# Per-language adapter with layer norm: each batch's W1 copied on chip and held stationary, x ring of nine pairs, one scaling per pair moved off VectorE

## The chip, the core and the metric

The kernel runs on one core of one Trainium2 chip. The metric is the device time of one execution in microseconds, the median of several. TensorE (PE) does the matrix products, VectorE (DVE), ScalarE (ACT) and GpSimd (POOL) the elementwise work, and SyncE (SP) issues nearly all DMAs. GpSimd can't read the matmul banks (PSUM); VectorE and ScalarE can. In this document a *pair* is two batches; there are 64.

## The reference, cut to what matters

There are 128 batches of x, each 128 rows by 512 columns, and ten languages. Every batch has a language id, which picks its W1 (512 x 128), b1, W2 (128 x 512), b2, gamma and beta. All is float32.

```python
h = relu(einsum('bsh,bha->bsa', x, W1[ids]) + b1[ids])
y = x + einsum('bsa,bah->bsh', h, W2[ids]) + b2[ids]
mean, var = mean(y, -1), var(y, -1)
out = x + (y - mean) * rsqrt(var + 1e-5) * gamma[ids] + beta[ids]
```

## The kernel before

All tables of all ten languages stay on chip in SBUF; the language of a batch is a register value that each engine loads from `lang_ids` (L156 to L160) and uses as an offset into the tables. Per pair the work goes like this.

- SP (L206 to L250) loads x of a pair (512 KB, `x_io`, a ring of 24 slots, that is 12 pairs) and stores the result from the same slots. In the steady state it waits for `out_ready` of pair p, issues the store, then waits for the store of pair p - 1 and issues the load of pair p + 11 (L239 to L244).
- PE, step p (L455 to L476): the second product of pair p - 3 (`second_product`, L420, three matmuls of 512 columns per batch, float32 split into a high and a low part: h_high x W2_high, h_high x W2_low, h_low x W2_high), the eight transposes of x of pair p + 1 (`turn_x`, L388), the two transposes of h of pair p - 1 (`turn_h`, L407), and the first product of pair p (`first_product`, L397). There x_T is the stationary operand and W1, at an offset from a register, the moving one, so h comes out with rows in partitions and has to be transposed. Each batch starts with a bf16 matmul that brings b1 (L399).
- ACT, step p (L351, L379 to L385): squares with their sum for both banks of pair p - 3 and the square root (`square_pair`, L343), the copy of transposed x out of PSUM (`copy_x`, L318), the copy of h before it is transposed (`copy_h`, L331, with the relu) and of its high part after (`high_h`, L336).
- DVE (`norm_and_seed`, L599): for pair n it scales both banks, (y - mean) x gamma, in place in PSUM (`scale_pair`, L559), inverts the deviation (L564), finishes both batches, bank x rstd + x, into x's slots (`finish_pair`, L572), makes the low part of h of pair n + 2 (`low_h`, L529), and seeds the banks of pair n + 2 with x + b2, with the row sum (`seed_pair`, L540; inputs `x_io` and `b2_all`, both in SBUF). There are four banks `ps_y`, two pairs' worth.
- POOL (`add_beta`, L288): for pair n it waits for both seeds and for the transposes of x, makes the two means (L292), and adds beta to x in its slots, twice (L295; inputs `x_io` and `beta_all`).

So DVE's order is written out by hand, and PE, ACT, POOL and SP follow it through semaphores. Before that there is a prologue of about 37 us, in which the tables are loaded, gamma and beta are spread to all partitions by matmuls (L438), and W2 is made free of its mean and split in two parts. `w2_high` is made by ACT (L328), `w2_low` by DVE (`low_w2`, L520, from the staged W2 and `w2_high`, both in SBUF). POOL cuts beta and b2 into three bf16 parts in that time (`cut_in_three`, L271).

Of the kernel before, what the change touches and what calls it, by code (L numbers as in the profile page):

```python
# [13 lines left out]
SLOTS = 24  # L14
Y_BANKS = 4
H_PAIRS = 6
FIRST = 3
# [4 lines left out]
def build(nc, x, ids, w1, b1, w2, b2, gamma, beta, out):  # L22
# [11 lines left out]
    x_pairs = x.rearrange("(n b) s h -> s n b h", b=2)  # L34
    out_pairs = out.rearrange("(n b) s h -> s n b h", b=2)
# [6 lines left out]
    assert FIRST + 2 <= H_PAIRS  # L42

    with ExitStack() as ctx:  # L44
# [10 lines left out]
        w1_all = sb("w1_all", [128, L, C, A], F32)  # L55
        w2_high = sb("w2_high", [128, L, H], F32R)
# [9 lines left out]
        cut = sb("cut", [128, 3, H], BF16)  # L66
# [4 lines left out]
        b1_parts = sb("b1_parts", [128, A], BF16)  # L71
        later_part = sb("later_part", [128, 2], F32)
# [3 lines left out]
        ids_raw = sb("ids_raw", [1, B], I32)  # L76
        ids_fix = sb("ids_fix", [1, 2, B], F32)
        lang_ids = sb("lang_ids", [1, B], I32)
        eps = sb("eps", [128, 1], F32)
        over_h = sb("over_h", [128, L], F32)  # L80
# [4 lines left out]
        h_rows = sb("h_rows", [128, 2, 2, A], F32)  # L85
# [4 lines left out]
        mean = sb("mean", [128, SLOTS], F32)  # L90
# [6 lines left out]
        ps_h = psum("ps_h", [128, H], F32)  # L97
        ps_hT = psum("ps_hT", [128, H], F32)
# [8 lines left out]
        s_w1 = sem("s_w1")  # L107
        s_w2 = [sem(f"s_w2_{n}") for n in range(W_CHUNKS)]
# [8 lines left out]
        over_h_ready = sem("over_h_ready")  # L117
# [27 lines left out]
        h_rows_ready = sem("h_rows_ready")  # L145
        h_turned = sem("h_turned")
# [46 lines left out]
        spread_banks = ps_y + [ps_h, ps_hT]  # L193
# [13 lines left out]
        def _(sp):  # L207
# [3 lines left out]
            sp.dma_start(ids_raw[:, :], ids.rearrange("(a b) -> a b", a=1)).then_inc(s_ids, 16)  # L211
# [7 lines left out]
            for n in range(W2_AHEAD):  # L219
                load_w2(n)  # L220
# [9 lines left out]
            for p in range(4, X_FIRST):  # L230
# [3 lines left out]
                load_x(p)  # L234
            for n in range(W_CHUNKS):
# [17 lines left out]
        def _(pool):  # L253
# [5 lines left out]
            for g in range(3):  # L259
                nc.gpsimd.affine_select(out=pick_row[:, :], in_=pick_row[:, :], compare_op=ALU.not_equal, fill=1.0,  # L260
                                        base=-L * g, pattern=[[-1, L]], channel_multiplier=1).then_inc(pick_step, 1)
                pool.wait_ge(pick_step, g + 1)

# [4 lines left out]
            nc.gpsimd.memset(over_h[:, :], 1.0 / H).then_inc(over_h_ready, 1)  # L268
            nc.gpsimd.memset(neg_over_h[:, :], -1.0 / H).then_inc(over_h_ready, 1)
# [12 lines left out]
            pool.wait_ge(parts_zero, 2)  # L282
# [5 lines left out]
            def add_beta(n):  # L288
                langs = langs_of(pool, n)
                pool.wait_ge(seeded, 2 * n + 2)  # L290
                pool.wait_ge(x_turned, 2 * n + 2)
                nc.gpsimd.tensor_tensor(stats(mean, n), stats(row_sum, n), over_h[:, 0:2], ALU.mult).then_inc(mean_ready, 1)  # L292
                for b in range(2):
                    t = 2 * n + b
                    nc.gpsimd.tensor_tensor(x_slot(t), x_slot(t), of_lang(beta_all, langs[b]), ALU.add)\  # L295
                        .then_inc(x_beta_ready, 1)

            pool.wait_ge(ids_ready, 1)
            pool.wait_ge(over_h_ready, 2)
            pool.wait_ge(spread_act, len(by_act))  # L300
            pool.wait_ge(spread_dve, len(by_dve))
            for n in range(PAIRS):
                add_beta(n)

        @block.scalar
        def _(act):
# [24 lines left out]
            def copy_h(p):  # L331

                act.wait_ge(h_summed, p + 1)
                nc.scalar.activation(flat(h_rows[:, p % 2, :, :]), pair_of(ps_h), ACT.Relu).then_inc(h_rows_ready, 1)  # L334

            def high_h(p):  # L336
                act.wait_ge(h_turned, p + 1)
                if p >= H_PAIRS:
                    act.wait_ge(adapted, 2 * (p - H_PAIRS) + 2)
                nc.scalar.copy(flat(h_high[:, p % H_PAIRS, :, :]), pair_of(ps_hT)).then_inc(h_high_ready, 1)  # L340
# [9 lines left out]

            def step(p):  # L351
# [3 lines left out]
                if p > 0:  # L355
                    high_h(p - 1)
                copy_h(p)
# [14 lines left out]
            copy_h(0)  # L372
            copy_x(2)
            high_h(0)
            high_w2(3)
            copy_h(1)
            high_w2(4)
            step(2)
            for p in range(FIRST, PAIRS):  # L379
                square_pair(p - FIRST)  # L380
                step(p)
            square_pair(PAIRS - FIRST)
            high_h(PAIRS - 1)
            for n in range(PAIRS - FIRST + 1, PAIRS):
                square_pair(n)  # L385

        @block.tensor
        def _(pe):  # L388
            def turn_x(t):
                if t % 2 == 0:  # L390
                    pe.wait_ge(x_loaded[t // 2 % X_PAIRS], x_loads(t // 2))
                for c in range(C):
                    last = nc.tensor.transpose(ps_T[:, t % 2, c, :], x_io[:, t % SLOTS, c * 128:(c + 1) * 128],  # L393
# [3 lines left out]
            def first_product(t, lang):  # L397
                part = pair_of(ps_h)[:, (t % 2) * A:(t % 2 + 1) * A]
                nc.tensor.matmul(part, of_lang(pick, lang), b1_parts[:, :], start=True, stop=False)  # L399
                for c in range(C):  # L400
                    last = nc.tensor.matmul(part, x_T[:, t % 4, c, :],  # L401
                                            w1_all[:, bass.ds(lang, 1), c, :].rearrange("p o a -> p (o a)"),
                                            start=False, stop=(c == C - 1))
                if t % 2 == 1:
                    last.then_inc(h_summed, 1)

            def turn_h(p):  # L407
                pe.wait_ge(h_rows_ready, p + 1)
                if p > 0:
                    pe.wait_ge(h_low_ready, p)  # L410
                for b in range(2):
                    last = nc.tensor.transpose(pair_of(ps_hT)[:, b * S:(b + 1) * S], h_rows[:, p % 2, b, :],  # L412
                                               identity[:, :])
                last.then_inc(h_turned, 1)
# [21 lines left out]
            pe.wait_ge(parts_zero, 2)  # L436
# [14 lines left out]
            pe.wait_ge(b1_parts_ready, 1)  # L451
            pe.wait_ge(spread_act, len(by_act))
            pe.wait_ge(spread_dve, len(by_dve))
            pe.wait_ge(s_w1, 16 * W_CHUNKS)
            for p in range(PAIRS):  # L455
# [10 lines left out]
                if p > 0:  # L466
                    turn_h(p - 1)
                for b in range(2):
                    first_product(2 * p + b, langs[p][b])
# [7 lines left out]
            for n in range(PAIRS - FIRST, PAIRS):  # L477
                for b in range(2):
                    second_product(2 * n + b, langs[n][b])
                if n == PAIRS - FIRST:  # L480
                    turn_h(PAIRS - 1)

        @block.vector
        def _(dve):
            nc.vector.memset(parts[:, :], 0.0).then_inc(parts_zero, 1)
            nc.vector.memset(b1_parts[:, :], 0.0).then_inc(parts_zero, 1)
            dve.wait_ge(s_ids, 16)
# [16 lines left out]

            dve.wait_ge(later_part_ready, 1)
            dve.wait_ge(parts_zero, 2)
# [126 lines left out]
```

## Time and profile before

| what | value |
|---|---|
| median of 3 runs | 325.21 us (325.19 to 325.84) |
| the profiled execution, first to last instruction (span) | 323.8 us |
| around the span, against the median | 1.4 us |
| PE busy | 301.9 us, 93% |
| DVE busy | 307.6 us, 95% |
| ACT busy | 230.4 us, 71% (a square: 0.69 us, 128 of them) |
| POOL busy | 185.7 us, 57% |
| DMA | 75.7 MB, 234 GB/s on average |

The span is what the profiler saw from the first to the last instruction; the execution's own time isn't given separately, so the prediction sums up to the span and adds what lies between it and the median. Busy times of PE count matmuls that overlap in the pipeline as one. An idle time in a row is that of the engine just before the operation, with what ended it behind the arrow. Starts of neighbouring operations tell what each costs; records overlap a little.

### The profile page before, as it was taken

The numbers are of one execution on the slowest core, as the hardware profiler recorded it, in microseconds if no ns is written. First come the engines' busy times: TensorE is split into PE (matmuls) and PEld (weight loads), VectorE is DVE, ScalarE is ACT, GpSimd is POOL, SyncE is SP. The second block draws the span as 40 slices with busy tenths as digits, with TensorE's granted clock in tenths as the row PEclk, the third lists the DMA queues.
The fourth block names the chain that finished last, engine by engine and source line by source line (L and its number), as shares of the span: only waits on it lengthen the run. The fifth ranks groups of instructions, "written<-read, shape, count | busy, mean of one in ns | idle before, by whom it ended". The sixth has DMA issues, their size and how long they took to land. (4 is left out here: it accounts for less than half of the span.)

```text
span 323.8 us, 8068 instructions
## 1 busy us (share of the span) xinstructions
PE 301.9 (93%) x2200; PEld 272.8 (84%) x2200; DVE 307.6 (95%) x679; ACT 230.4 (71%) x541; POOL 185.7 (57%) x217
## 2 busy tenths in 40 slices
PE   1659999999999999999999999999999999999962
PEld 1239899999999999999999999999999999999941
DVE  5687999999999999999999999999999999999996
ACT  3956677777777777877778777787777877778752
POOL 2960755556655566555665556655566555665553
PEclk9877999999999999999999999999999999999995
DMA  5999988766766667676776676766667666433324
GB/s 160 302 356 428 379 291 273 236 228 231 257 232 227 228 229 263 223 233 226 230 256 232 228 231 227 261 236 221 231 225 262 221 234 232 160 132 134 130 108 152
DMA packets 41711, 75.69 MB, mean 234 GB/s; under 512 B 2253, under 2 KB 7404, under 8 KB 41542
## 3 DMA queue, kind: packets, MB, share of 16 engines
q1 hardware_dynamic: 41571, 75.04, 68.5%
q8 instruction: 21, 0.34, 0.4%
q14 instruction: 20, 0.16, 0.1%
q10 hardware_dynamic: 99, 0.14, 0.1%
HBM read 41.62 MB, written 33.55 MB: 232 GB/s over the span
## 5 line engine op out<-in xcount | busy, mean ns | idle before, releaser
L295 POOL TENSOR_TENSOR x_io<-x_io,beta_all 128x512 f32<-128x512 f32 x128 | 161.2, 1280 | 0.0
L401 PE MATMUL ps_h<-w_all,x_T 128*128 x1024 | 137.0, 284 | 0.0
L401 PEld LDWEIGHTS ps_h<-w_all,x_T 128*128 128x128 f32 x1024 | 126.1, 194 | 1.6
L345 ACT ACTIVATE cut<-ps_y,row_sum 128x512 bf16<-128x512 f32 x128 | 88.0, 688 | 24.0 <-PE ps_y L428 24.0
L572 DVE SCALAR_TENSOR_TENSOR x_io<-ps_y,rstd,x_io 128x512 f32<-128x512 f32 x128 | 90.2, 747 | 2.5 <-DVE rstd L564 0.3
L559 DVE SCALAR_TENSOR_TENSOR ps_y<-ps_y,mean,gamma_all 128x512 f32<-128x512 f32 x128 | 90.8, 754 | 0.8 <-ACT cut L345 0.6
L292 POOL TENSOR_TENSOR mean<-row_sum,over_h 128x2 f32<-128x2 f32 x64 | 12.9, 201 | 125.6 <-DVE ps_y L540 113.6
L540 DVE SCALAR_TENSOR_TENSOR ps_y<-x_io,b_all 128x512 f32<-128x512 f32 x124 | 83.1, 713 | 0.0
L393 PE MATMUL ps_T<-identity,x_io 128*128 128x128 f32 x512 | 68.2, 277 | 10.0 <-DMA x_io<-in_x 10.0
L393 PEld LDWEIGHTS ps_T<-identity,x_io 128*128 128x128 f32 x512 | 61.1, 143 | 19.1 <-issue 10.4
L322 ACT COPY x_T<-ps_T 128x1024 f32<-128x1024 f32 x64 | 63.7, 995 | 8.2 <-PE ps_T L393 8.2
L334 ACT ACTIVATE h_rows<-ps_h 128x256 f32<-128x256 f32 x64 | 24.8, 387 | 52.0 <-PE ps_h L401 52.0
L428 PE MATMUL ps_y<-w_high,h_high 128*128 x128 | 56.4, 440 | 3.4 <-DVE ps_y L540 3.0
L428 PE MATMUL ps_y<-w_high,h_low 128*128 x128 | 51.1, 399 | 0.0
L428 PE MATMUL ps_y<-w_low,h_high 128*128 x128 | 50.9, 398 | 0.0
L428 PEld LDWEIGHTS ps_y<-w_high,h_high 128*128 128x128 f32 x128 | 24.5, 192 | 7.1 <-issue 4.2
L428 PEld LDWEIGHTS ps_y<-w_high,h_low 128*128 128x128 f32 x128 | 24.3, 190 | 5.7
L529 DVE SCALAR_TENSOR_TENSOR h_low<-ps_hT,h_high 128x256 fp32r<-128x256 f32 x64 | 26.6, 415 | 1.9 <-ACT h_high L340 1.9
L399 PE MATMUL ps_h<-b_parts,pick 128*128 128x128 bf16 x128 | 28.2, 220 | 0.0
L428 PEld LDWEIGHTS ps_y<-w_low,h_high 128*128 128x128 f32 x128 | 24.6, 192 | 2.6
L345 ACT ACTIVATION_READ_ACCUMULATOR cut<-ps_y,row_sum 128x1 f32 x128 | 24.6, 192 | 0.0
L412 PE MATMUL ps_hT<-identity,h_rows 128*128 128x128 f32 x128 | 24.5, 273 | 0.1
(60 smaller groups left out, 173.6 us busy)
## 6 DMA issues: line engine op xcount, KB each, us to landing
x_io<-in_x SPq DMA_DIRECT2D x64, 512.0 KB, 4.4
out<-x_io SPq DMA_DIRECT2D x63, 512.0 KB, 3.0
x_io<-in_L_cond_W SPq DMA_DIRECT2D x5, 512.0 KB, 7.2
w_all<-in_L_cond_W SPq DMA_DIRECT2D x5, 512.0 KB, 8.9
b_all<-in_L_cond_b SPq DMA_DIRECT2D x1, 2560.0 KB, 15.7
out<-x_io SPq DMA_DIRECT2D x2, 256.0 KB, 2.0
x_io<-in_L_cond_gamma SPq DMA_DIRECT2D x1, 60.0 KB
x_io<-in_L_cond_beta ACTq DMA_DIRECT2D x1, 60.0 KB
```

Of the source, the lines that this page charges most:

```text
L295: nc.gpsimd.tensor_tensor(x_slot(t), x_slot(t), of_lang(beta_all, langs[b]), ALU.add)\
L322: nc.scalar.copy(x_T[:, slots, :, :].rearrange("p b c s -> p (b c s)"), ps_T[:, :, :, :].rearrange("p b c s -> p (b c s)")).then_inc(x_T_r ...
L334: nc.scalar.activation(flat(h_rows[:, p % 2, :, :]), pair_of(ps_h), ACT.Relu).then_inc(h_rows_ready, 1)
L345: nc.scalar.activation(squares[:, t % 2, :], ps_y[t % Y_BANKS][:, :], ACT.Square, scale=-float(H), bias=stat(row_sum, t), accum_out=stat(s ...
L393: last = nc.tensor.transpose(ps_T[:, t % 2, c, :], x_io[:, t % SLOTS, c * 128:(c + 1) * 128], identity[:, :])
L399: nc.tensor.matmul(part, of_lang(pick, lang), b1_parts[:, :], start=True, stop=False)
L401: last = nc.tensor.matmul(part, x_T[:, t % 4, c, :], w1_all[:, bass.ds(lang, 1), c, :].rearrange("p o a -> p (o a)"), start=False, stop=(c ...
L428: last = nc.tensor.matmul(bank, h_part[:, h, b, :], of_lang(w2_part, lang), start=False, stop=False, skip_group_check=True)
L529: nc.vector.scalar_tensor_tensor(flat(h_low[:, p % H_PAIRS, :, :]), pair_of(ps_hT), 1.0, flat(h_high[:, p % H_PAIRS, :, :]).bitcast(F32), ...
L540: nc.vector.scalar_tensor_tensor(ps_y[t % Y_BANKS][:, :], x_slot(t), 1.0, of_lang(b2_all, langs[b]), ALU.mult, ALU.add, accum_out=stat(row ...
L559: nc.vector.scalar_tensor_tensor(bank, bank, stat(mean, t), of_lang(gamma_all, langs[b]), ALU.subtract, ALU.mult).then_inc(scaled, 1)
L572: nc.vector.scalar_tensor_tensor(x_slot(t), ps_y[t % Y_BANKS][:, :], stat(rstd, t), x_slot(t), ALU.mult, ALU.add).then_inc(out_ready, 1)
```

## The change

W1 is now read from HBM so that partition p holds rows 4p to 4p + 3 of each language's W1, in one run of 2 KB. The transposes of x pick every fourth column to match (column 4p + c of x goes to partition p of part c). SP copies the W1 of each batch from the table `w1_all` to one of eight slots `w1_stage` (four pairs), two DMAs of 256 KB per pair, six pairs ahead. In the first product the slot is the stationary operand and x_T the moving one, so h comes out already transposed, with relu put into the copy of the high part and into the low part. `copy_h` and `turn_h` are gone, and there are two banks `ps_h`. One bf16 matmul per pair brings b1, with its moving operand a table `is_lang` of ones and zeros that is spread over 256 columns. The ring of x has 18 slots, the second product runs 2 steps behind instead of 3.

DVE scales only the first bank of a pair. For the second, ACT writes y - mean to SBUF (`centred`, two slots), POOL multiplies it by gamma in place, and DVE finishes from there, one pair later. The seed of a second bank then waits for the centring and not for the finish. POOL's order per pair is the means, beta for the first batch, gamma for the second of the pair before, beta for the second batch.

```diff
-SLOTS = 24
+SLOTS = 18
-H_PAIRS = 6
-FIRST = 3
+H_PAIRS = 3
+STAGE_PAIRS = 4
+STAGE_AHEAD = 6
+FIRST = 2
+    w1_rows = w1.rearrange("l (p c) a -> p l c a", c=C)
...
+            def stage_w1(q):
+                langs = langs_of(sp, q)
+                if q >= STAGE_PAIRS:
+                    sp.wait_ge(h_summed, q - STAGE_PAIRS + 1)
+                for b in range(2):
+                    sp.dma_start(w1_stage[:, 2 * (q % STAGE_PAIRS) + b, :, :], w1_all[:, bass.ds(langs[b], 1), :, :])\
+                        .then_inc(w1_staged[q % STAGE_PAIRS], 16)
...
-                sp.dma_start(w1_all[:, langs, :, :], w1[langs].rearrange("l (c p) a -> p l c a", p=128)).then_inc(s_w1, 16)
+                sp.dma_start(w1_all[:, langs, :, :], w1_rows[:, langs, :, :]).then_inc(s_w1, 16)
+            sp.wait_ge(ids_ready, 1)
+            sp.wait_ge(s_w1, 16 * W_CHUNKS)
+            stage_w1(0)
             load_x(1)
+            stage_w1(1)
             for n in range(W2_AHEAD, W_CHUNKS):
                 load_w2(n)
             load_x(2)
-            load_x(3)
+            stage_w1(2)
+            stage_w1(3)
             sp.dma_start(b2_all[:, :, :], b2.partition_broadcast(128)).then_inc(s_b2, 16)
...
             for p in range(PAIRS - 1):
+                if p + STAGE_AHEAD < PAIRS:
+                    stage_w1(p + STAGE_AHEAD)
                 sp.wait_ge(out_ready, 2 * p + 2)
...
-            def add_beta(n):
+            def add_beta(t, lang):
+                pool.wait_ge(x_turned, t + 1)
+                nc.gpsimd.tensor_tensor(x_slot(t), x_slot(t), of_lang(beta_all, lang), ALU.add).then_inc(x_beta_ready, 1)
+
+            def gain(n, lang):
+                pool.wait_ge(centred_ready, n + 1)
+                nc.gpsimd.tensor_tensor(centred[:, n % 2, :], centred[:, n % 2, :], of_lang(gamma_all, lang), ALU.mult)\
+                    .then_inc(gained, 1)
...
             for n in range(PAIRS):
-                add_beta(n)
+                langs[n] = langs_of(pool, n)
+                mean_of_pair(n)
+                add_beta(2 * n, langs[n][0])
+                if n > 0:
+                    gain(n - 1, langs[n - 1][1])
+                add_beta(2 * n + 1, langs[n][1])
+            gain(PAIRS - 1, langs[PAIRS - 1][1])
...
+            def centre(n):
+                t = 2 * n + 1
+                act.wait_ge(adapted, t + 1)
+                act.wait_ge(mean_ready, n + 1)
+                if n >= 2:
+                    act.wait_ge(out_ready, 2 * (n - 2) + 2)
+                nc.scalar.activation(centred[:, n % 2, :], ps_y[t % Y_BANKS][:, :], ACT.Identity,
+                                     bias=stat(neg_mean, t)).then_inc(centred_ready, 1)
...
-                    last = nc.tensor.transpose(ps_T[:, t % 2, c, :], x_io[:, t % SLOTS, c * 128:(c + 1) * 128],
+                    last = nc.tensor.transpose(ps_T[:, t % 2, c, :], x_slot(t).rearrange("s (p c) -> s c p", c=C)[:, c, :],
                                                identity[:, :])
...
+            def first_products(p):
+                bank = pair_of(ps_h[p % 2])
+                if p >= 2:
+                    pe.wait_ge(h_low_ready, p - 1)
+                nc.tensor.matmul(bank.rearrange("a (b s) -> a b s", b=2), b1_parts[:, :],
+                                 is_lang[:, 2 * p:2 * p + 2].unsqueeze(2).broadcast_to([128, 2, S]), start=True, stop=True)
+                pe.wait_ge(w1_staged[p % STAGE_PAIRS], 32 * (p // STAGE_PAIRS + 1))
                 for b in range(2):
+                    for c in range(C):
+                        last = nc.tensor.matmul(bank[:, b * S:(b + 1) * S],
+                                                w1_stage[:, 2 * (p % STAGE_PAIRS) + b, c, :],
+                                                x_T[:, (2 * p + b) % 4, c, :],
+                                                start=False, stop=False, skip_group_check=True)
+                last.then_inc(h_summed, 1)
...
+            def finish_second(n):
+                t = 2 * n + 1
+                dve.wait_ge(rstd_ready, n + 1)
+                dve.wait_ge(gained, n + 1)
+                dve.wait_ge(x_beta_ready, t + 1)
+                nc.vector.scalar_tensor_tensor(x_slot(t), centred[:, n % 2, :], stat(rstd, t), x_slot(t),
+                                               ALU.mult, ALU.add).then_inc(out_ready, 1)
...
+            def norm_and_seed(n):
+                scale_first(n, langs[n][0])
                 if n + 2 < PAIRS:
                     langs[n + 2] = langs_of(dve, n + 2)
+                if n > 0:
+                    finish_second(n - 1)
                 invert_pair(n)
+                finish_first(n)
                 if n + 2 < PAIRS:
                     seed_pair(n + 2, langs[n + 2])
+                    low_h(n + 2)
```

## Rows read from the trace of the kernel before

**Rows 1.** Windows: busy us (count) of PE, PEld, DVE, ACT, POOL; clock, DMA share, GB/s.

```profile
32.00:48.00 16.00, 15.63 (x121) 14.48 (x120) 15.14 (x36) 12.12 (x28) 10.46 (x12) 1.00 0.92 341
60.00:270.00 210.00, 210.00 (x1590) 194.27 (x1589) 207.83 (x467) 155.57 (x373) 124.70 (x140) 1.00 0.70 235
```

**Rows 2.** Timeline of one pair, all engines: start us, us, engine, line, what.

```profile
151.83 0.48 PE L428 MATMUL ps_y<-w_high,h_high 128*128 x1
...
153.31 1.04 PE L393 MATMUL ps_T<-identity,x_io 128*128 128x128 f32 x8
...
153.79 1.42 DVE L559 SCALAR_TENSOR_TENSOR ps_y<-ps_y,mean,gamma_all 128x512 f32<-128x512 f32 x2
153.94 0.19 POOL L292 TENSOR_TENSOR mean<-row_sum,over_h 128x2 f32<-128x2 f32 x1 [1.83 <-DVE ps_y L540]
...
154.09 2.51 POOL L295 TENSOR_TENSOR x_io<-x_io,beta_all 128x512 f32<-128x512 f32 x2
...
154.18 0.38 PE L412 MATMUL ps_hT<-identity,h_rows 128*128 128x128 f32 x2
...
154.40 0.22 PE L399 MATMUL ps_h<-b_parts,pick 128*128 128x128 bf16 x1
...
155.11 0.16 DVE L564 RECIPROCAL rstd<-std 128x2 f32<-128x2 f32 x1
...
156.32 0.48 PE L428 MATMUL ps_y<-w_high,h_high 128*128 x1
...
156.96 0.69 DVE L540 SCALAR_TENSOR_TENSOR ps_y<-x_io,b_all 128x512 f32<-128x512 f32 x1
```

**Rows 3.** Timeline of DVE: first scaling, and the last two pairs.

```profile
37.01 0.76 DVE L559 SCALAR_TENSOR_TENSOR ps_y<-ps_y,mean,gamma_all 128x512 f32<-128x512 f32 x1 [0.55 <-ACT cut L345]
...
315.42 1.41 DVE L559 SCALAR_TENSOR_TENSOR ps_y<-ps_y,mean,gamma_all 128x512 f32<-128x512 f32 x2
...
319.76 1.41 DVE L572 SCALAR_TENSOR_TENSOR x_io<-ps_y,rstd,x_io 128x512 f32<-128x512 f32 x2
```

**Rows 4.** Groups of POOL, 60 to 270 us: busy us, mean ns, idle before, releaser.

```profile
L295 POOL TENSOR_TENSOR x_io<-x_io,beta_all 128x512 f32<-128x512 f32 x94 | 118.0, 1276 | 0.0
L292 POOL TENSOR_TENSOR mean<-row_sum,over_h 128x2 f32<-128x2 f32 x46 | 9.0, 195 | 84.4 <-DVE ps_y L540 84.4
```

**Rows 5.** Timeline of PE in the prologue: the first eight transposes.

```profile
6.51 1.94 PE L393 MATMUL ps_T<-identity,x_io 128*128 128x128 f32 x8 [6.51 <-DMA x_io<-in_x]
```

**Rows 6.** The page, part 6: the DMA of x and its landing.

```profile
x_io<-in_x SPq DMA_DIRECT2D x64, 512.0 KB, 4.4
```

**Rows 7.** Timelines of POOL and DVE in the prologue, single operations in order of time.

```profile
16.02 1.15 POOL L277 TENSOR_TENSOR b_rows<-b_rows,b_cut 30x512 f32<-30x512 f32 x1
...
18.19 0.74 DVE L523 SCALAR_TENSOR_TENSOR w_low<-x_io,w_neg_mean,w_high 128x512 fp32r<-128x512 f32 x1
...
18.89 1.70 POOL L277 TENSOR_TENSOR b_rows<-b_rows,b_cut 30x512 f32<-30x512 f32 x1
...
19.51 1.64 DVE L523 SCALAR_TENSOR_TENSOR w_low<-x_io,w_neg_mean,w_high 128x512 fp32r<-128x512 f32 x1
...
33.68 0.58 POOL L292 TENSOR_TENSOR mean<-row_sum,over_h 128x2 f32<-128x2 f32 x1 [12.07 <-DVE ps_y L550]
...
34.12 0.75 DVE L523 SCALAR_TENSOR_TENSOR w_low<-x_io,w_neg_mean,w_high 128x512 fp32r<-128x512 f32 x1
...
34.22 1.79 POOL L295 TENSOR_TENSOR x_io<-x_io,beta_all 128x512 f32<-128x512 f32 x1
```

**Rows 8.** Window at the end, columns as in rows 1, and PE's last wait.

```profile
306.00:324.00 18.00, 8.80 (x42) 6.19 (x39) 15.03 (x32) 7.66 (x23) 7.98 (x9) 0.73 0.39 145
...
315.04 0.77 PE L428 MATMUL ps_y<-w_high,h_high 128*128 x1 [2.79 <-DVE ps_y L540]
```

**Rows 9.** Timeline of SP's issues of W1, and DVE's sum of the third W2 chunk.

```profile
4.14 10.56 SPq L223 DMA_DIRECT2D w_all<-in_L_cond_W  x5
...
22.91 1.22 DVE L515 TENSOR_REDUCE w_sum<-x_io 128x2 f32<-128x1024 f32 x1 [0.75 <-DMA x_io<-in_L_cond_W]
```

More of the change, by code:

```diff
@@ L55, in build @@
         w1_all = sb("w1_all", [128, L, C, A], F32)
+        w1_stage = sb("w1_stage", [128, 2 * STAGE_PAIRS, C, A], F32)
         w2_high = sb("w2_high", [128, L, H], F32R)
@@ L96, in build @@
         ps_T = psum("ps_T", [128, 2, C, S], F32)
-        ps_h = psum("ps_h", [128, H], F32)
-        ps_hT = psum("ps_hT", [128, H], F32)
+        ps_h = [psum(f"ps_h{i}", [128, H], F32) for i in range(2)]
         ps_y = [psum(f"ps_y{i}", [128, H], F32) for i in range(Y_BANKS)]
@@ L107, in build @@
         s_w1 = sem("s_w1")
+        w1_staged = [sem(f"w1_staged{i}") for i in range(STAGE_PAIRS)]
         s_w2 = [sem(f"s_w2_{n}") for n in range(W_CHUNKS)]
@@ L227, in _ @@
             load_x(2)
-            load_x(3)
+            stage_w1(2)
+            stage_w1(3)
             sp.dma_start(b2_all[:, :, :], b2.partition_broadcast(128)).then_inc(s_b2, 16)
-            for p in range(4, X_FIRST):
+            for p in range(3, X_FIRST):
                 if p == ROWS_PAIR:
@@ L234, in _ @@
                 load_x(p)
+            for q in range(STAGE_PAIRS, STAGE_AHEAD):
+                stage_w1(q)
             for n in range(W_CHUNKS):
@@ L286, in _, with mean_of_pair @@
             cut_in_three(b2_rows[:, :], b2_cut[:, 1, :], parts[0:3 * L, 2 * H:3 * H], 4, b2_parts_ready)
-            def add_beta(n):
-                langs = langs_of(pool, n)
+            def mean_of_pair(n):
                 pool.wait_ge(seeded, 2 * n + 2)
[L291 to L296, printed above, removed]
+                nc.gpsimd.tensor_tensor(stats(neg_mean, n), stats(row_sum, n), neg_over_h[:, 0:2], ALU.mult)\
+                    .then_inc(mean_ready, 1)
+            def add_beta(t, lang):
[5 more added lines that the diff above has]
+                    .then_inc(gained, 1)
             pool.wait_ge(ids_ready, 1)
-            pool.wait_ge(over_h_ready, 2)
+            pool.wait_ge(neg_over_h_ready, 1)
             pool.wait_ge(spread_act, len(by_act))
             pool.wait_ge(spread_dve, len(by_dve))
+            langs = {}
             for n in range(PAIRS):
-                add_beta(n)
+                langs[n] = langs_of(pool, n)
[5 more added lines that the diff above has]
+            gain(PAIRS - 1, langs[PAIRS - 1][1])
         @block.scalar
@@ L371, in _ @@
             high_w2(2)
-            copy_h(0)
-            copy_x(2)
             high_h(0)
             high_w2(3)
-            copy_h(1)
+            copy_x(2)
+            high_h(1)
             high_w2(4)
-            step(2)
             for p in range(FIRST, PAIRS):
                 square_pair(p - FIRST)
+                centre(p - FIRST)
                 step(p)
-            square_pair(PAIRS - FIRST)
-            high_h(PAIRS - 1)
-            for n in range(PAIRS - FIRST + 1, PAIRS):
+            for n in range(PAIRS - FIRST, PAIRS):
                 square_pair(n)
+                centre(n)
         @block.tensor
@@ L465, in _ @@
                     turn_x(2 * p + 3)
[L466 to L469, printed above, removed]
+                first_products(p)
                 if p < PAIRS - 1:
@@ L551, in seed_early, with scale_first @@
                                                    accum_out=stat(row_sum, t)).then_inc(seeded, 1)
-            def scale_pair(n, langs):
+            def scale_first(n, lang):
+                t = 2 * n
+                bank = ps_y[t % Y_BANKS][:, :]
                 dve.wait_ge(mean_ready, n + 1)
-                for b in range(2):
-                    t = 2 * n + b
-                    bank = ps_y[t % Y_BANKS][:, :]
-                    dve.wait_ge(squared, t + 1)
-                    nc.vector.scalar_tensor_tensor(bank, bank, stat(mean, t), of_lang(gamma_all, langs[b]),
-                                                   ALU.subtract, ALU.mult).then_inc(scaled, 1)
+                dve.wait_ge(squared, t + 1)
+                nc.vector.scalar_tensor_tensor(bank, bank, stat(neg_mean, t), of_lang(gamma_all, lang),
+                                               ALU.add, ALU.mult).then_inc(scaled, 1)
             def invert_pair(n):
```

119 lines of the change are left out of this document (55 added, 64 removed).

## The prediction

> **What bounds the kernel now.** I read the page's busy shares first, then the windows by stage, one pair's timeline, and POOL's groups with their idle time. In the long middle two engines are full: PE is busy 210.0 of 210 us and DVE 207.8, while ACT has 155.6, POOL 124.7 and the DMA engines 0.70 [rows 1]. The timeline of one pair [rows 2] shows the period: the second product starts at 151.83 and again at 156.32, so a pair takes 4.49 us on both engines. The span agrees: the first scaling starts at 37.01, that of pair 62 at 315.42, and 62 periods of 4.49 are 278.4 us [rows 3]. So the time is 37.0 us of start, 62 periods, and 8.4 us of end, 323.8 us together; the median of the runs, 325.21, is 1.4 us more, which I add at the end.
>
> The reader should look at one more thing: what POOL does with its idle time. In the middle it waits 84.4 us for DVE's seeds [rows 4]. In the pair of [rows 2] its chain starts at 153.94, right behind the seeds, and is over at 156.60, just before DVE's next seeds start at 156.96. So the seeds, DVE operations with both inputs in SBUF, never run beside a POOL operation. The other big DVE operations of the pair take one input from PSUM.
>
> **The change, part by part.**
> PE: two transposes of h go: from 154.18 to 154.40, 0.22 us [rows 2]. Of two b1 matmuls one is left, with 256 moving columns. Sixteen products and two b1 take 154.40 to 156.32, 1.92 us; at the transposes' spacing of 0.11 (0.87 for eight) the products are 1.76, so a b1 matmul is some 0.08. The merged one costs between one and two of these: I take 0.05 saved (bounds 0 and 0.08). The sixteen products swap operands, same count, same 128 columns. PE: 4.49 - 0.27 = 4.22. The transposes of x now read every fourth element; no row has such a read, so its bounds are nothing and a halved rate: eight transposes in 1.94 us in the prologue against 1.04 in the pair [rows 2, 5]. I take nothing, the price of the nearest row of the same instruction, and keep 0.9 for the range.
> DVE: scaling two banks is 153.79 to 155.11, 1.32 us; one goes, 0.66. The other finish only changes its input from bank to SBUF. DVE: 4.49 - 0.66 = 3.83.
> ACT: loses the 0.39 us of h_rows, gains the centring, priced by the squares: 155.6 us over 46.8 pairs is 3.33. The squares are 0.69 by the trace's table in the section on the profile, so 3.63 us a pair, not the bound.
> POOL: now 2.66 us a pair (0.15 for the mean and 2.51 for two additions of beta); one more operation of the same form at 1.25 makes 3.91.
> DMA: a pair moves 1.05 MB now and 1.57 MB with the two W1 slices. At the rate of the fullest stretch shown (341 GB/s at a share of 0.92, so 371) that is 4.24 us; at the rate of the middle (235 at 0.70, so 336) it is 4.68 [rows 1]. I take 4.24, because a queue that is never empty is the first case. On SP the W1 slices are issued six pairs ahead and the loads of x seven or eight, both over 15 us against a landing of 4.4 us [rows 6], so the ring of 9 costs nothing; if that cover were gone a pair would wait those 4.4 us. The slices' two issues and language loads are priced by the 10.56 us of five W1 issues [rows 9] at most, 4.2 us for two, likelier tenths; nothing on SP is late by either, as it works pairs ahead.
>
> Alone, then, the period would be 4.3. What decides against it is how POOL and DVE run together. **The collision.** The new finish reads `centred` and x, both in SBUF; the seeds still do. The trace has such pairs in the prologue, in w2_low (both inputs in SBUF) beside POOL [rows 7]. Alone w_low takes 0.75 us. The third one started at 19.51, under a POOL tensor_tensor that ran 18.89 to 20.60, and took 1.64, so it began its work at 20.40, 0.19 before POOL's end. That POOL operation took 1.70 where its like took 1.15 (it started under the second w_low). The small mean took 0.58 where 0.20 is usual, and the first beta addition 1.79 instead of 1.28 [rows 4], ending 0.52 later because the w_low at 34.12 ran until 34.87. So each waits for nearly all of the other. Against it stands one case: the first w_low ran at its usual 0.74 beside a POOL tensor_scalar; the new work is all tensor_tensor.
> The Trainium skill, SBUF — State Buffer, Who interferes with whom, states that a VectorE instruction with two SBUF inputs and a GpSimd one that reads SBUF take turns for the whole instruction. By its whole instruction the period would be the serial sum of the second rival below; the rows agree but for the small overlap at each change of hands.
>
> Price: when DVE's operation slips between two of POOL's, POOL's counts 1.28 - 0.19 = 1.09 and DVE's 0.74 - 0.14 = 0.60 (POOL began 0.14 before w_low's end, 34.73 against 34.87). Together 1.69 against 1.25 for POOL alone: each costs 0.44. A pair has three, two seeds and the new finish, and POOL has no free time left to avoid them: 3.91 + 3 x 0.44 = 5.23. DVE fits that order: after each of its three it finds 0.85 to 1.0 us of other work (low_h and scaling, or inversion and finish) while POOL's takes 1.09. I take 5.25. PE at 4.22 of it idles 1 us a pair; its granted clock was full from 32 to 48 us [rows 1] and fell from 2.4 to 1.2 GHz at the end, around an idle of 2.79 us (0.73 on average there) [rows 8], so I leave it at full speed; at half speed nothing here would hold.
>
> Start: W1 in 2 KB rows makes its five issues shorter than the 10.56 us of before, which end at 14.70, and x of pair 1 stood behind them [rows 9]. Now SP waits for all of W1 and issues the first slices before it. 4.2 MB stand ahead in the queue, 11.3 us at 371 GB/s from 2.8, so it goes on at 14 to 16. Behind that wait stand x1, three W2 chunks and b2. The third W2 chunk then has four transfers of 1.4 us, landing near 22 to 23, and it was first used at 22.91. I keep 37.0, within 2 us.
> End: pairs 62 and 63 have no seeds. POOL does 0.15 + 4 x 1.25 and one slip of 0.44, DVE the last finish 0.75, and from the end of the last finish (321.17) to the span's end were 2.66: 9.0 us.
> **Sum**: 37.0 + 62 x 5.25 + 9.0 = 371.5, with 1.4 it is 373.
>
> **The rivals.**
> 1. No collision between these (faster): the seeds and the new finish run beside POOL freely, for instance because what was seen holds for w_low alone. Then 4.3, PE and DMA: 37.0 + 266.6 + 8.6 (no slip) + 1.4 = 314. If only the new finish collides, POOL has 4.35 and the time is 317. It decides below a period of 4.48, where the sum is that of now. For: the seeds write PSUM, and no row has one beside POOL. Against: what they share with w_low is both inputs in SBUF, and four operations of the prologue agree. Chance 0.17.
> 2. Serial: hand-overs don't alternate, or overlap nothing: 3.91 + 3 x 0.66 = 5.89, 413 us. For: POOL's next operation starts 0.03 before the last ends and may come first. Against: the rows' overlap. Chance 0.12.
> 3. DMA: 4.68 a pair, 337 us, if the collision is slight. For: three streams on one queue, share 0.70 now. Against: the full stretch. Chance 0.05.
> 4. Strided transposes: PE 4.22 + 0.9 = 5.1, 363 us. Only this and the collision together leave about the forecast. Chance 0.06 as the one that decides. The Trainium skill, SBUF — State Buffer, Door 1, says that reads which go to a new 16-byte line each time pay; four fp32 apart is such a step, and no run so far shows it.
> 5. Partly colliding, landing within 0.2% of now (what a measurement can tell): 0.03.
>
> **How the numbers follow.** The forecast has 0.57: slower in total 0.57 + 0.12 + 0.05 + 0.06 = 0.80; faster 0.17, same 0.03. The range takes rivals 3 and 4 at its low end and 2 at its high end: 336 to 414.
>
> **What the profile after would show.** Right: period 5.2 to 5.3; POOL busy (its waits counted in) near 100%; L540's successors and the new finish over 1 us instead of 0.71 and 0.75; beta additions 1.4 to 1.8 instead of 1.28; PE idle about 1 us a pair, waiting for seeds or low h; DMA share about 0.8. Wrong: those operations at their old durations; PE full at 4.2 (rival 1), or full at 5.1 with transposes 0.22 apart (4); DMA share 1 with PE waiting for w1_stage (3).

## The result, and the profile after

The changed kernel takes 401.19 us (median of 4 runs, 400.69 to 401.78) against 325.23 for the kernel before on the same chip: 1.2325 times as long, with an interval of 1.2303 to 1.2347. The prediction was 373 us, with a range of 336 to 414.

The middle first: windows of the kernel after, with the columns of [rows 1].

```profile
60.00:270.00 210.00, 169.91 (x1166) 152.96 (x1167) 199.97 (x339) 136.51 (x302) 183.62 (x152) 1.00 0.80 283
```

PE went from 210 to 170, POOL rose from 125 to 184, and the DMA engines have 0.80. DVE is recorded busy for 200, but an operation that another engine holds up counts as busy for all of that time, so this is no measure of its work. The clock stayed at the higher level of 2.4 GHz (granted share 1.00), although PE now waits in each pair. The groups of the same stretch (columns of [rows 4]) name the operations that grew:

```profile
L323 POOL TENSOR_TENSOR x_io<-x_io,beta_all 128x512 f32<-128x512 f32 x76 | 116.5, 1533 | 0.0
L588 DVE SCALAR_TENSOR_TENSOR ps_y<-x_io,b_all 128x512 f32<-128x512 f32 x75 | 88.5, 1221 | 8.7 <-DVE x_io L618 8.7
L328 POOL TENSOR_TENSOR centred<-centred,gamma_all 128x512 f32<-128x512 f32 x38 | 66.0, 1736 | 0.0
L626 DVE SCALAR_TENSOR_TENSOR x_io<-centred,rstd,x_io 128x512 f32<-128x512 f32 x38 | 45.6, 1200 | 0.0
...
L618 DVE SCALAR_TENSOR_TENSOR x_io<-ps_y,rstd,x_io 128x512 f32<-128x512 f32 x38 | 28.6, 751 | 1.4
...
L318 POOL TENSOR_TENSOR neg_mean<-row_sum,neg_over_h 128x2 f32<-128x2 f32 x38 | 7.4, 195 | 27.1 <-DVE ps_y L588 27.1
```

The seed (L588) is the same instruction as before's L540 and now takes 1.22 us on average. The finish from SBUF (L626) takes 1.20, the finish from a bank (L618) still 0.75. Gamma on POOL takes 1.74. POOL nevertheless waits 27.1 us for the second seed; its busy time and this wait fill the whole stretch, as the prediction's sign of being right had it. The timeline of one pair, DVE, POOL and PE, shows how (start us, us, engine, line, what):

```profile
200.20 1.19 DVE L626 SCALAR_TENSOR_TENSOR x_io<-centred,rstd,x_io 128x512 f32<-128x512 f32 x1
...
200.80 1.74 POOL L328 TENSOR_TENSOR centred<-centred,gamma_all 128x512 f32<-128x512 f32 x1
...
202.47 0.70 DVE L588 SCALAR_TENSOR_TENSOR ps_y<-x_io,b_all 128x512 f32<-128x512 f32 x1 [0.22 <-DVE x_io L618]
202.50 1.79 POOL L323 TENSOR_TENSOR x_io<-x_io,beta_all 128x512 f32<-128x512 f32 x1
...
203.09 1.76 DVE L588 SCALAR_TENSOR_TENSOR ps_y<-x_io,b_all 128x512 f32<-128x512 f32 x1
...
204.78 0.41 DVE L574 SCALAR_TENSOR_TENSOR h_low<-ps_h,h_high 128x256 fp32r<-128x256 f32 x1
204.99 0.19 POOL L318 TENSOR_TENSOR neg_mean<-row_sum,neg_over_h 128x2 f32<-128x2 f32 x1 [0.69 <-DVE ps_y L588]
...
205.14 1.28 POOL L323 TENSOR_TENSOR x_io<-x_io,beta_all 128x512 f32<-128x512 f32 x1
...
205.44 0.50 PE L468 MATMUL ps_y<-w_high,h_high 128*128 x1 [1.06 <-DVE h_low L574]
...
205.77 1.20 DVE L626 SCALAR_TENSOR_TENSOR x_io<-centred,rstd,x_io 128x512 f32<-128x512 f32 x1
```

L626 starts at 200.20 and again at 205.77: the period is 5.57 us. Three DVE operations with both inputs in SBUF (L626 and two of L588) take turns with three large POOL operations. The second seed ran 1.76 because it could begin only when POOL's beta ended. POOL then stood idle for 0.69 us, because its next operation, the mean, needs that very seed. PE waited 1.06 us for the low part of h, which stands behind the seed on DVE.

Start and end, DVE's timeline:

```profile
27.41 1.22 DVE L560 TENSOR_REDUCE w_sum<-x_io 128x2 f32<-128x1024 f32 x1 [5.87 <-DMA x_io<-in_L_cond_W]
...
43.86 0.75 DVE L606 SCALAR_TENSOR_TENSOR ps_y<-ps_y,neg_mean,gamma_all 128x512 f32<-128x512 f32 x1
...
389.28 0.74 DVE L606 SCALAR_TENSOR_TENSOR ps_y<-ps_y,neg_mean,gamma_all 128x512 f32<-128x512 f32 x1
```

The first scaling starts at 43.86 instead of 37.01 [rows 3], that of pair 62 at 389.28: 62 periods of 5.571. From there to the end are 9.6 us. 43.9 + 62 x 5.571 + 9.6 = 398.9, the span. Against before's span of 323.8 the 75.1 us more are 67.0 of period, 6.9 of start and 1.2 of end.

### The profile page after: what moved, and what is told of

It is laid out like the page before. It is cut to its first block and busy times, and to the rows that moved or that the text cites. A ratio compares the mean times of both kernels' runs of the same rounds, so it can differ in the third digit from the quotient of the medians.

```text
span 398.9 us, 7375 instructions
## 1 busy us (share of the span) xinstructions
PE 302.7 (76%) x2007; PEld 267.0 (67%) x2008; DVE 365.2 (92%) x619; ACT 250.2 (63%) x541; POOL 324.3 (81%) x281
## 5 line engine op out<-in xcount | busy, mean ns | idle before, releaser
L323 POOL TENSOR_TENSOR x_io<-x_io,beta_all 128x512 f32<-128x512 f32 x128 | 195.4, 1526 | 0.0
L588 DVE SCALAR_TENSOR_TENSOR ps_y<-x_io,b_all 128x512 f32<-128x512 f32 x124 | 147.9, 1234 | 13.9 <-DVE x_io L618 13.9
L450 PE MATMUL ps_h<-x_T,w_stage 128*128 128x128 f32 x1024 | 126.9, 278 | 0.0
L450 PEld LDWEIGHTS ps_h<-x_T,w_stage 128*128 128x128 f32 x1024 | 121.5, 195 | 0.8
L328 POOL TENSOR_TENSOR centred<-centred,gamma_all 128x512 f32<-128x512 f32 x64 | 110.1, 1720 | 0.9 <-ACT centred L395 0.9
L436 PEld LDWEIGHTS ps_T<-identity,x_io 128*128 128x128 f32 x512 | 73.1, 209 | 21.5 <-issue 16.5
L626 DVE SCALAR_TENSOR_TENSOR x_io<-centred,rstd,x_io 128x512 f32<-128x512 f32 x64 | 76.0, 1188 | 1.0 <-POOL centred L328 0.9
L618 DVE SCALAR_TENSOR_TENSOR x_io<-ps_y,rstd,x_io 128x512 f32<-128x512 f32 x64 | 48.1, 751 | 2.3
L606 DVE SCALAR_TENSOR_TENSOR ps_y<-ps_y,neg_mean,gamma_all 128x512 f32<-128x512 f32 x64 | 47.6, 744 | 0.3 <-ACT cut L382 0.3
L395 ACT ACTIVATE centred<-ps_y,neg_mean 128x512 f32<-128x512 f32 x64 | 42.7, 668 | 0.0
L574 DVE SCALAR_TENSOR_TENSOR h_low<-ps_h,h_high 128x256 fp32r<-128x256 f32 x64 | 26.5, 414 | 0.0
```

The lines of the kernel that those rows point to most:

```text
L328: nc.gpsimd.tensor_tensor(centred[:, n % 2, :], centred[:, n % 2, :], of_lang(gamma_all, lang), ALU.mult)\
L395: nc.scalar.activation(centred[:, n % 2, :], ps_y[t % Y_BANKS][:, :], ACT.Identity, bias=stat(neg_mean, t)).then_inc(centred_ready, 1)
L436: last = nc.tensor.transpose(ps_T[:, t % 2, c, :], x_slot(t).rearrange("s (p c) -> s c p", c=C)[:, c, :], identity[:, :])
L450: last = nc.tensor.matmul(bank[:, b * S:(b + 1) * S], w1_stage[:, 2 * (p % STAGE_PAIRS) + b, c, :], x_T[:, (2 * p + b) % 4, c, :], start=F ...
L588: nc.vector.scalar_tensor_tensor(ps_y[t % Y_BANKS][:, :], x_slot(t), 1.0, of_lang(b2_all, langs[b]), ALU.mult, ALU.add, accum_out=stat(row ...
L606: nc.vector.scalar_tensor_tensor(bank, bank, stat(neg_mean, t), of_lang(gamma_all, lang), ALU.add, ALU.mult).then_inc(scaled, 1)
```

## The experiments

Each was compared with the kernel before on the same chip, except the small kernel without an adapter, which ran once. "Period" is a 62nd of the time from the first scaling to that of pair 62. The edits are shortened; names in a row and words in brackets stand for the lines of the change.

**The split of the scaling alone.** The kernel before, with only the second scaling divided among ACT, POOL and DVE as in the change (ring of 11 pairs to make room for `centred`).

```diff
-SLOTS = 24
+SLOTS = 22
-scale_pair / finish_pair / add_beta
+scale_first, finish_second(n - 1), finish_first, centre, gain   (as in the change)
```

> The kernel before with only the scaling of the second bank moved (centring on ScalarE, gamma on GpSimd, finish from SBUF one pair later), no W1 slots, ring of 11 pairs, low h ahead of the seeds. Theory: taking turns costs the same as in the changed kernel, 5.2 to 5.6 us a pair, 370 to 398 us, with second seed, new finish and gamma long. Rival A: near 325, PE at 4.49. Rival B: near 325.

400.76 us, ratio 1.2287 (1.2228 to 1.2346), period 5.68; the expected range ended at 398. This half alone makes the whole loss, with a DMA share of only 0.56. Its start is that of before (first scaling at 37.17), and its period is 0.11 longer than the changed kernel's, so that the two times agree only by chance to 0.4 us. Its groups of DVE and POOL in the middle:

```profile
L573 DVE SCALAR_TENSOR_TENSOR ps_y<-x_io,b_all 128x512 f32<-128x512 f32 x74 | 90.3, 1259 | 0.3 <-issue 0.3
...
L303 POOL TENSOR_TENSOR centred<-centred,gamma_all 128x512 f32<-128x512 f32 x37 | 63.7, 1722 | 0.0
L611 DVE SCALAR_TENSOR_TENSOR x_io<-centred,rstd,x_io 128x512 f32<-128x512 f32 x37 | 57.0, 1540 | 0.0
```

**The W1 half alone.** The changed kernel with both scalings and finishes back on DVE.

```diff
-scale_first, finish_second(n - 1), finish_first, centre, gain
+scale_pair, finish_pair, both betas on POOL   (as before the change)
```

> The W1 half of the change alone: slots, swapped operands, ring of 9, but both scalings of a pair on VectorE and only two beta additions on GpSimd. Theory (VectorE operations with both inputs in SBUF and GpSimd's take turns): the long operations go away, the seeds are at 0.7 us again and GpSimd's at 1.28. VectorE has its 4.49 us plus the 0.22 us that the seed now waits right behind the finish: 4.7 us a pair, 335 to 342 us. Rival A (the W1 copies, half as much DMA again, slow the operations): seeds and beta additions stay long, above 380 us. Rival B (the change's PE order and low h after the seeds are what costs): above 380 us too, with operations at their old durations.

330.23 us, ratio 1.0144 (1.0097 to 1.019), period 4.43, below the expected 335 to 342; the 0.22 us of waiting that was expected in each pair did not come. Both rivals wanted above 380 us and fall. With `low_h` ahead of the seeds:

```diff
-                    seed_pair(n + 2, langs[n + 2])
-                    low_h(n + 2)
+                    low_h(n + 2)
+                    seed_pair(n + 2, langs[n + 2])
```

> As w1_only, with low h ahead of the seeds as in the kernel before. Theory: the 0.22 us wait in front of the first seed is covered again; VectorE bound at 4.43 to 4.49 us a pair, PE at 4.35: 320 to 327 us. Rival A: above 380. Rival B: near 325, but then w1_only must be above 380.

329.1 us, ratio 1.0106 (1.0061 to 1.0151), period 4.425. The period is the expected one; the time is 2 us above its range, which the late start below accounts for. Its window, and SP's issues in the prologue:

```profile
60.00:270.00 210.00, 209.89 (x1485) 192.13 (x1484) 208.31 (x477) 146.22 (x336) 126.41 (x142) 1.00 1.01 354
```

```profile
4.13 3.36 SPq L241 DMA_DIRECT2D w_all<-in_L_cond_W  x5
18.44 1.21 SPq L234 DMA_DIRECT2D w_stage<-w_all  x2
```

So the W1 half gains only 0.07 us a pair, since DVE's own work is 4.42 against PE's former 4.49. It loses 7.2 us at the start (first scaling at 44.21): SP waits from 7.5 to 18.44 for the whole of W1. The DMA engines ran at 354 GB/s and a share of 1.01 without anybody waiting for them in the middle.

**The copies.** The changed kernel without W1 copies past the first four pairs; later pairs use the slices of the first four. It leaves out 120 of the 128 copies.

```diff
-            for q in range(STAGE_PAIRS, STAGE_AHEAD):
-                stage_w1(q)
...
-                if p + STAGE_AHEAD < PAIRS:
-                    stage_w1(p + STAGE_AHEAD)
...
-                pe.wait_ge(w1_staged[p % STAGE_PAIRS], 32 * (p // STAGE_PAIRS + 1))
+                pe.wait_ge(w1_staged[p % STAGE_PAIRS], 32)
```

> The changed kernel without the W1 copies after the first four pairs; later pairs use the W1 of those four, so that part of the computation is not the reference's. Theory: within 1% of the changed kernel, 397 to 403 us, same long operations. Rival A: near or below 325 us.

401.0 us, ratio 1.2294, period 5.58, DMA share 0.56. The copies cost the changed kernel nothing in the middle.

**POOL's multiplication away.** The changed kernel without `gain`; the second finish waits for the centring. Gamma is left out for every second batch.

```diff
-                if n > 0:
-                    gain(n - 1, langs[n - 1][1])
-                dve.wait_ge(gained, n + 1)
+                dve.wait_ge(centred_ready, n + 1)
```

> The changed kernel without GpSimd's multiplication by gamma for the second batch of each pair (left out of the result); the new finish, from SBUF, stays. Theory: GpSimd has 2.66 us and at most three changes of hands at 0.44, 3.98 a pair, VectorE 3.83 + 0.22 and one or two blocked operations: 4.4 to 4.9 us a pair, 320 to 352 us. Rival B (order of low h and PE's wait for it): no change, near 400 us.

340.31 us, ratio 1.0414 (1.0377 to 1.0451), period 4.61, the median one 4.55. Its groups:

```profile
L323 POOL TENSOR_TENSOR x_io<-x_io,beta_all 128x512 f32<-128x512 f32 x92 | 136.5, 1504 | 0.2 <-issue 0.2
...
L585 DVE SCALAR_TENSOR_TENSOR ps_y<-x_io,b_all 128x512 f32<-128x512 f32 x92 | 62.0, 715 | 10.4 <-DVE x_io L615 10.4
L623 DVE SCALAR_TENSOR_TENSOR x_io<-centred,rstd,x_io 128x512 f32<-128x512 f32 x45 | 52.6, 1168 | 1.9 <-POOL x_io L323 0.7 <-issue 0.6
```

With POOL free again in part of the pair, the seeds are back at 0.715 us. What collides is the finish from SBUF, which slips between the two betas. The middle gives back 0.96 us a pair of the 1.08 by which 5.57 stands above 4.49. Of this run's own loss of 15 us against the kernel before, half is its period, 0.12 longer, and half its start (first scaling at 44.83).

**The price of a collision by itself.** No adapter at all: 12 operations of 128x512 float32 per stage on DVE, alone or beside 12 on POOL. The arithmetic of the reference is left out.

```diff
+for each stage: DVE scalar_tensor_tensor, inputs two SBUF tiles or one SBUF and one PSUM, output SBUF or PSUM
+                POOL nothing, or tensor_tensor on two SBUF tiles, or tensor_scalar on one
```

> No adapter at all: stages of twelve VectorE operations x 1.5 + b (128x512) and twelve GpSimd operations, alone and together. Order of the stages: VectorE SBUF+SBUF to SBUF alone; GpSimd add alone; both together; VectorE SBUF+SBUF to PSUM with the add; VectorE PSUM+SBUF to SBUF with the add; then the same three forms with GpSimd's tensor_scalar, which reads one tensor. Theory: alone 0.65 and 1.25 us each; together with the add both VectorE forms that read two SBUF tensors take 1.69 us for one of each in alternation, about 20 us for twelve of each, wherever they write; the PSUM+SBUF form doesn't slow. Rival A: both at their own pace, 15 us for the stage. Rival C (only results written to SBUF collide): the form that writes PSUM doesn't slow.

```profile
36.34 11.74 DVE L76 SCALAR_TENSOR_TENSOR v_out<-a,b 128x512 f32<-128x512 f32 x7
37.50 25.29 POOL L57 TENSOR_TENSOR g_out<-c,d 128x512 f32<-128x512 f32 x15
```

Seven DVE operations, the last of them 1.74 long, in 11.74 us: they start every 1.667 us. Alone they start every 0.602, POOL's alone every 1.219. So the two engines alternate strictly, one operation each, and an alternated pair costs 1.667 against 1.82 for the sum of both: 0.15 overlap. It is the same where DVE writes to PSUM, as the seeds do. With one DVE input from PSUM neither slows the other (0.598 apart). Beside POOL's `tensor_scalar` DVE's operations start 0.602 and 1.013 us apart in turn, two of them to one of POOL's, so that one holds DVE up for only 0.41.

**Order of low_h in the changed kernel.** PE waits for `h_low`, so a rival cause was DVE's order. The edit is that of the second W1 run, made in the changed kernel.

> The changed kernel with low h ahead of the seeds. Theory (taking turns bounds the pair): at most the 0.22 us wait of the first seed is won, 5.2 to 5.57 us a pair, 380 to 402 us. Rival B (PE waits 1.06 us a pair for low h, which now stands behind a seed of 1.76 us): PE gets it 2.5 us earlier, its wait goes and the period falls to PE's 4.35, below 330 us.

405.31 us, ratio 1.2438 (1.2399 to 1.2478), period 5.64: 4 us worse, and above the expected 402. PE's wait for `h_low` is gone and no time with it, so it is no cause. PE now waits for the seeds instead (34.5 us in the middle), and the finish from SBUF grows from 1.20 to 1.54 us.

**The mean off POOL.** The two means of a pair go to ACT, and POOL's first beta waits for the first seed only. Nothing on POOL then waits for the second seed until its own beta.

```diff
-                pool.wait_ge(seeded, 2 * n + 2)
-                nc.gpsimd.tensor_tensor(stats(neg_mean, n), stats(row_sum, n), neg_over_h[:, 0:2], ALU.mult)
+            (add_beta) pool.wait_ge(seeded, t + 1)
+            (ACT, square_pair) nc.scalar.activation(stats(neg_mean, n), stats(row_sum, n), ACT.Copy, scale=-1.0 / H)
```

> The changed kernel with the two means of a pair made on ScalarE, so that GpSimd's first beta addition of a pair waits for the first seed alone and not for the second. In the changed kernel GpSimd stands idle 0.69 us a pair for the second seed. Theory (the pair is a closed chain of alternating VectorE and GpSimd operations, and that wait and the mean are 0.15 + 0.3 to 0.7 us of its 5.57): 4.9 to 5.3 us a pair, 358 to 384 us. Rival (serial use of GpSimd and VectorE as such makes 5.57, the wait is slack): no change, 398 to 404 us.

373.69 us, ratio 1.1457 (1.1417 to 1.1498), period 5.13. Its window and POOL's group:

```profile
60.00:270.00 210.00, 184.93 (x1271) 166.52 (x1271) 199.20 (x367) 152.59 (x368) 209.21 (x124) 1.00 0.86 307
```

```profile
L319 POOL TENSOR_TENSOR x_io<-x_io,beta_all 128x512 f32<-128x512 f32 x83 | 143.5, 1747 | 0.8 <-DVE ps_y L586 0.8
```

POOL is full now, at 209.2 of 210, and the period is three alternated pairs, 3 x 1.667 = 5.00, and 0.13. The second seed and the first beta addition of the next pair, in this run:

```profile
201.53 1.76 DVE L586 SCALAR_TENSOR_TENSOR ps_y<-x_io,b_all 128x512 f32<-128x512 f32 x1
...
202.70 1.72 POOL L319 TENSOR_TENSOR x_io<-x_io,beta_all 128x512 f32<-128x512 f32 x1
```

Beta ends 1.13 us after the seed (204.42 against 203.29). In the changed kernel it ended 1.57 after it (206.42 against 204.85). The 0.44 between them is the whole gain of the period.

**Contiguous transposes.** The second W1 run with the old layout of W1, so that the transposes read 128 neighbouring columns.

```diff
-x_slot(t).rearrange("s (p c) -> s c p", c=C)[:, c, :]
+x_slot(t)[:, c * 128:(c + 1) * 128]
-w1.rearrange("l (p c) a -> p l c a", c=C)
+w1.rearrange("l (c p) a -> p l c a", p=128)
```

> As w1_only_low_first, with the old layout of W1 and so transposes that read neighbouring columns. Theory: the transposes go back from 0.12 to 0.11 us each, PE from 4.35 to 4.27; VectorE still bounds, so within 0.5% of w1_only_low_first. If PE bounds there it is up to 0.08 us a pair faster, 5 us; the start may be 1 to 3 us later, as W1 lands in 512 B pieces.

331.14 us, ratio 1.0161 (1.013 to 1.0191), period 4.424. The middle is the same; the first scaling comes 2.0 us later (46.25), which is what this run is longer by. The weight loads of the transposes, first strided, then contiguous:

```profile
L431 PEld LDWEIGHTS ps_T<-identity,x_io 128*128 128x128 f32 x383 | 53.8, 208 | 3.8
```

```profile
L431 PEld LDWEIGHTS ps_T<-identity,x_io 128*128 128x128 f32 x384 | 44.8, 140 | 6.6
```

The stride costs 68 ns in each load, most of it hidden: eight transposes take 0.95 us instead of 0.88. In a kernel that DVE bounds that is nothing. The Trainium skill, SBUF — State Buffer, Door 1, says that each read that crosses to a new 16-byte line pays; the load agrees, the period doesn't feel it.

**The start.** The second W1 run with x1, x2 and the W2 chunks issued before SP waits for W1.

```diff
-            sp.wait_ge(s_w1, 16 * W_CHUNKS)
-            stage_w1(0)
             load_x(1)
             for n in range(W2_AHEAD, W_CHUNKS):
                 load_w2(n)
             load_x(2)
+            sp.wait_ge(s_w1, 16 * W_CHUNKS)
+            stage_w1(0)
```

> As w1_only_low_first, with x of pairs 1 and 2 and the last three W2 chunks issued before SP waits for W1, not behind that wait. Theory (the W1 half of the change wins 0.07 us a pair, 4.42 against 4.49, and loses some 7 us at the start because VectorE gets the third W2 chunk at 26.9 instead of 22.9 and PE gets x late): the first scaling comes at 37 to 41 us instead of 44.2, 319 to 325 us in all. Rival (the late start is the W1 copies' own time in the queue): 328 to 330 us, as before the edit.

326.11 us (12 runs), ratio 1.0018 (1.0001 to 1.0035); first scaling at 39.84, so 4.4 us of the lost 7.2 come back there. The first three periods, 6.49, 4.82 and 4.55, then lose 2.6 of them again, and the span falls by only 1.8 (326.8 to 325.0); the time is 1 us above its expected range. What is left over before's 37.01 shows in PE's waits:

```profile
25.68 3.78 PE L445 MATMUL ps_h<-x_T,w_stage 128*128 128x128 f32 x16 [3.62 <-DMA w_stage<-w_all]
37.10 0.79 PE L463 MATMUL ps_y<-w_high,h_high 128*128 x1 [3.93 <-DVE w_low L563]
```

**W1 without a table.** The second W1 run with each batch's slice loaded from HBM right into its slot. The table is gone, so the ring of x has room for 12 pairs again; slices are issued five pairs ahead, the first of them among the W2 chunks.

```diff
-SLOTS = 18
+SLOTS = 24
-STAGE_AHEAD = 6
+STAGE_AHEAD = 5
-w1_all[:, bass.ds(langs[b], 1), :, :]
+w1_rows[:, bass.ds(langs[b], 1), :, :]
-            for n in range(W_CHUNKS): (load w1_all); sp.wait_ge(s_w1, 16 * W_CHUNKS)
```

> As w1_only_low_first (both scalings on VectorE), but W1 of each batch comes from HBM straight into its slot; there is no W1 table on chip and no wait for it, and the ring of x has 12 pairs again. Theory (the middle is bound by VectorE at 4.42 us a pair, and the late start of the W1 half is the table's 2.6 MB and the wait for it): the first scaling at 34 to 38 us, 62 x 4.42 behind it, 314 to 321 us, 1 to 3% below the kernel before. Rival (the third stream from HBM does not fit in the time: 1.57 MB a pair at 336 GB/s are 4.68 us): DMA share 1.0, PE waits for the slots or x, 330 to 340 us.

319.12 us (6 runs, three of 317.3 to 317.9 and three of 320.3 to 320.8, of which one is the profiled run), ratio 0.9788 (0.975 to 0.9827): faster than both kernels, by 1.7 to 2.5% against the kernel before. Its window:

```profile
60.00:270.00 210.00, 209.79 (x1484) 192.11 (x1483) 208.31 (x474) 146.76 (x336) 127.00 (x143) 1.00 0.99 353
```

The first slices are issued at 5.28 and the first scaling starts at 34.13, 2.9 us earlier than before; the period is 4.459 on average and 4.425 in the median pair. 2.9 + 62 x 0.031 = 4.8, and the span fell by 4.7 (323.8 to 319.1). The average stands above the median because of one period of 6.51, the first. DVE bounds the middle. The DMA engines are at 353 GB/s, a share of 0.99, and no engine waits for them there; how much room they have left no run shows (the kernel before moved 407 GB/s between 22 and 35 us, at a share of 1.03, the spread of b2 to all partitions among it).

## Why the prediction was right, and where its sizes were off

**The mechanism held.** DVE operations with two SBUF inputs and POOL's took turns. The split alone gives the whole loss, the changed kernel without POOL's multiplication gives nearly none of it in the middle, and the small kernel shows the alternation with nothing else around. Rival 1 (no collision, also for seeds into PSUM) falls with that. Rival 2 (5.89, no overlap) falls with the 0.15 overlap of each pair of operations. The period alone wouldn't refute it: with the small kernel's 0.602 and 1.219 a serial pair costs 3 x 1.82 and the mean, 5.61, close to the 5.57 that was measured.

**The price of one collision was right.** The prediction took 1.69 us for a POOL operation and the DVE operation between; the small kernel gives 1.667. The Trainium skill, SBUF — State Buffer, Who interferes with whom, lets such operations take turns whole; by that it would be the sum of 1.82. The measurement lies 0.15 below. By the same section of the Trainium skill this holds beside any GpSimd instruction that reads SBUF. Beside `tensor_scalar` the small kernel shows less, 0.41 us for every second operation of DVE, and the measurement decides.

**The mis-sized term is the period: 5.25 predicted, 5.57 measured, 62 x 0.32 = 20 us of the 28 missing.** The step that failed is "DVE fits that order": it let POOL be busy without a break, and asked only whether DVE finds other work between its three operations. It missed that POOL waits too. The mean waits for the second seed, the seed is held by POOL's own beta, and so POOL can't start anything when the seed ends. The loop, from the timeline: three alternated pairs make 5.00. From the seed's end to the end of beta behind it are 1.57 us, namely 0.14 to the mean, 0.15 for the mean and 1.28 for beta; where POOL's operation stands ready under the seed it is 1.13 (the run with the mean on ACT), which makes 0.44 more. So beta, when it starts from rest, costs 0.15 beyond what it costs in the alternation. The last 0.13 are there in both runs (5.13 with the mean on ACT); I put them down to the first seed, which waits for L618's finish (0.22 of DVE's idle, L588), and no run shows that piece alone. The prediction had the mean's 0.15 too, and 5.08 for its three pairs, 0.08 too much; what it had at nothing are the two waits and beta's start from rest. The 373.69 us of the run with the mean on ACT are the forecast's 373 by accident in part, since its start is 8 us later than the forecast had it and its period is 5.13.

**The start was mis-sized: 37.0 within 2, measured 43.9, 7 us.** The step was "it goes on at 14 to 16": the prediction took 371 GB/s for the 4.2 MB, the engines moved 284 on average from 2.8 to 18.3, and SP went on at 18.30. Then "landing near 22 to 23": the third W2 chunk was first used at 27.41 instead of 22.91 [rows 9], and the weight split behind it is a chain on DVE and ACT. It reached the first scaling 16.5 us later, before it was 14.1. The run with the loads moved ahead of the wait took 4.4 us of it back at the first scaling, 1.8 of them in the span, and the one without the table all of it. The end took 9.6 instead of 9.0, and around the span lay 2.3 us instead of 1.4 (0.5 of them because the profiled run, 400.69, isn't the median one). 19.9 + 6.9 + 0.6 + 0.9 make the 28.

**PE's own work** is 4.33 by the timeline, not 4.22: the second product 1.51, transposes 0.95 (0.87 predicted, the stride), b1 0.11, products 1.76. Rival 4 (5.1) falls: the stride costs 0.07 and not 0.9. It lay under the collision anyway.

**DMA, rival 3:** 4.68 a pair at 336 GB/s would have set the time. The W1 half alone held 4.425 with 354 GB/s and no wait, and leaving the copies out changed nothing. What was costed at nothing (the shorter ring of x, SP's issues in the middle) cost nothing there: in the middle no engine waits for x or a W1 slice.

**The clock** stayed at the upper level through 1.06 us of PE's idle in each 5.57, as taken.

## What to carry to other kernels

Before an elementwise operation goes from VectorE to GpSimd, count the VectorE operations of the period that have both inputs in SBUF: while GpSimd is busy, each costs 0.45 us more on its side here, so an engine that was busy for 59% of the middle had less room than that. A second input from PSUM avoids it.

When two engines take turns, look for an operation on the one that waits for the held-up operation of the other. Such a loop puts every hand-over into the period: here moving a mean of 0.2 us to a third engine took 27 us off.

A table of which each step needs one slice can be read slice by slice from HBM, if the DMA engines have the room: it saved the wait at the start that filling the table cost.

## What of the hardware was not expected

The alternation is strict. Twelve independent operations on each engine, with no semaphore between the engines, went one by one, 1.667 us a pair, and POOL never took two in a row although its next one stood ready. With `tensor_scalar` on POOL, VectorE got two in for one.

The mix of copies within SBUF, loads and stores ran at 354 to 358 GB/s through 210 us, above the 336 at which the kernel before would have been full by its own middle. So a rate divided by its busy share, 235 by 0.70 there, is no ceiling.

Which part of the 2.8 us between the first scalings of the run with the early loads (39.84) and the kernel before (37.01) belongs to the copy out of the table, and which to the prologue's collisions with POOL (a pair of `w_low` took 3.16 us there where 1.41 is usual), was not separated.
